# A recurrence stage on one core: VectorE's score spreading moved from behind the decay chain to ahead of it

## What is computed

```python
def step(state, inp):
    k_t, v_t, w_t, r_t = inp
    kv = k_t[..., :, None] * v_t[..., None, :]
    state = (1.0 - w_t)[..., :, None] * state + kv
    out = jnp.einsum('bhd,bhde->bhe', r_t, state)
    return (state, out)
...
y = outs.transpose(1, 0, 2, 3).reshape(Bv, Tv, Cv) @ Wo.T
x = x + y
...
# then, in the feed-forward part, a routing of each token on the signs of its normed row
tile_scores = input_sigs @ tile_sigs.T
tile_idx = jnp.argmax(jnp.where(in_cluster, tile_scores, -jnp.inf), axis=-1)
```

## Time and profile before

| | |
|---|---|
| time, median of 3 runs | 8956.1 us (8954.75 to 8961.61) |
| time of the profiled execution | 8956.13 us |
| its span | 8954.3 us |
| busy: PE, DVE, ACT, POOL | 7718.1 (86%), 7107.0 (79%), 4707.2 (53%), 5805.7 (65%) us |
| `core_phase` loop, 7107 to 8673 us: PE, DVE, ACT, POOL busy | 1241.11, 1350.70, 349.61, 755.26 us of 1566 |
| L1223 at 128x320, mean of 62 | 1534 ns |
| L1236, 124 instructions, mean | 690 ns |

### The profile page before, as it was taken

One profiled execution on the slowest core, in us unless ns is written; L12 is line 12 of the kernel. 1 busy time (PEld: TensorE's weight loads), 2 busy tenths in 40 slices (PEclk: granted clock), 3 DMA queues, 4 the chain that ended last, 5 costly groups with the idle time before them and its releaser, 6 DMA issues. The chain is left out here.

```text
span 8954.3 us, 223728 instructions
## 1 busy us (share of the span) xinstructions
PE 7718.1 (86%) x76550; PEld 5688.4 (64%) x76550; DVE 7107.0 (79%) x8782; ACT 4707.2 (53%) x10584; POOL 5805.7 (65%) x3304
## 2 busy tenths in 40 slices
PE   5659989999989899999999998899999877778774
PEld 3337777777777777777777776444444455555552
DVE  5549999999999999999999998323323488888876
ACT  4447777777777777777777776111111122222220
POOL 0019999999999999999999998000000144444444
PEclk8779999999999999999999999999999887777875
DMA  3340000000000000000000001122212211121115
GB/s 129 136 149 0 20 20 19 0 20 20 0 20 20 20 0 20 20 10 9 20 20 0 20 5 58 61 84 75 89 67 88 83 61 60 63 63 63 61 47 172
DMA packets 198781, 423.45 MB, mean 47 GB/s; under 512 B 22448, under 2 KB 48496, under 8 KB 183024
## 3 DMA queue, kind: packets, MB, share of 16 engines
q1 hardware_dynamic: 172768, 382.77, 12.7%
q10 hardware_dynamic: 25872, 38.80, 1.2%
HBM read 225.11 MB, written 196.41 MB: 47 GB/s over the span
## 5 line engine op out<-in xcount | busy, mean ns | idle before, releaser
L453 POOL TENSOR_TENSOR scan_hc<-scan_h,scan_cb 128x1024 f32<-128x1024 f32 x2048 | 4779.6, 2369 | 253.1 <-DMA scan_cb<-scratch_bc 117.6
L619 DVE TENSOR_TENSOR_SCAN scan_h<-scan_a,scan_carry,scan_u 128x512 f32<-128x512 f32 x4096 | 4801.9, 1261 | 156.1 <-PE scan_u L558 125.3
L558 PE MATMUL scan_u<-scan_dg,scan_v 64*128 64x128 f32 x32768 | 2391.7, 286 | 340.0 <-DVE scan_h L619 280.1
L504 ACT ACTIVATE scan_a<-scan_dt,scan_aneg 128x512 f32<-128x512 f32 x4096 | 2659.5, 708 | 44.4 <-issue 30.1
L558 PEld LDWEIGHTS scan_u<-scan_dg,scan_v 64*128 64x128 f32 x32768 | 2000.7, 188 | 820.0 <-DVE scan_h L619 538.1
L566 PE MATMUL scan_y<-scan_ident,scan_hc 128*128 128x128 f32 x16408 | 2250.4, 280 | 59.5 <-POOL scan_hc L453 33.6
L566 PEld LDWEIGHTS scan_y<-scan_ident,scan_hc 128*128 128x128 f32 x16408 | 1764.3, 141 | 309.7 <-POOL scan_hc L453 34.5
L475 ACT ACTIVATE scan_dg<-scan_half,scan_bt 128x64 f32<-128x64 f32 x4096 | 1138.7, 341 | 5.3 <-DVE scan_onward L602 5.2
L144 POOL TENSOR_TENSOR mid_r<-mid_ve,mid_half_neg 128x4 f32<-128x4 f32 x48 | 48.5, 1011 | 1269.0 <-DVE mid_ve L129 1269.0
L496 ACT ACTIVATE scan_carry<-scan_h,scan_onward 128x4 f32 (+1 forms) x1008 | 302.9, 301 | 1043.1 <-DVE scan_h L619 1043.1
L1223 DVE TENSOR_TENSOR core_rk<-core_rr,core_k 128x128 f32<-128x128 f32 (+7 forms) x512 | 409.0, 799 | 0.0
(11 more groups left out here) (211 smaller groups left out, 8209.8 us busy)
## 6 DMA issues: line engine op xcount, KB each, us to landing
scratch_y<-scan_yo ACTq DMA_DIRECT2D x17, 1024.0 KB, 4.7
pre_x<-in_x SPq DMA_DIRECT2D x16, 1024.0 KB, 6.9
scratch_z<-pre_zt SPq DMA_DIRECT2D x16, 1024.0 KB, 3.9
scratch_dt<-pre_dt SPq DMA_DIRECT2D x16, 1024.0 KB, 4.6
scratch_vr<-pre_vr ACTq DMA_DIRECT2D x16, 1024.0 KB, 4.7
scan_dt<-scratch_dt SPq DMA_DIRECT2D x16, 1024.0 KB, 5.3
scan_v<-scratch_vr SPq DMA_DIRECT2D x32, 512.0 KB, 7.7
scan_z<-scratch_z SPq DMA_DIRECT2D x16, 1024.0 KB, 10.7
```

The lines of the kernel that those rows point to most:

```text
L453: pool.tensor_tensor(hc[:, q].rearrange("p n (r j) -> p n r j", j=P), h[:, q].rearrange("p n (r j) -> p n r j", j=P), cb[:, bass.ds(b * NS ...
L504: ins = act.activation(a[:, q, n, :], dt[:, par, q, :], ACT.Exp, scale=aneg[:, q, bass.ds(m * 2 + n, 1)])
L558: mm = pe.matmul(u_ps[:, q % 2, g, k * HP:(k + 1) * HP, :], v[row, par, k, q, :], dg[row, buf, k], start=True, stop=True)
L619: ins = dve.tensor_tensor_scan(h[:, q, n, :], a[:, q, n, :], u_ps[:, q % 2, :, :, n].rearrange("p g t -> p (g t)"), carry[:, q, bass.ds(m ...
```

## The change

In VectorE's list `spread_scores`, with lead 2, is now written ahead of `decays`, with lead 3. Nothing else differs.

```diff
@@ -1259,7 +1259,7 @@
                 for e in range(2):
                     after.inc(dve.scalar_tensor_tensor(out=ext[:, e, :], in0=pen[:], scalar=mm2[:, e:e + 1], in1=ext[:, e, :], op0=ALU.min, op1=ALU.max))
                 after.wait(dve, i, after.n)
-            pipelined(dve, ITEMS, [(0, state), (0, norms), (3, decays), (2, spread_scores), (0, route)])
+            pipelined(dve, ITEMS, [(0, state), (0, norms), (2, spread_scores), (3, decays), (0, route)])
```

## The result

| | before | after |
|---|---|---|
| median | 8958.85 us (8954.75 to 8963.20, 4 runs) | 9076.86 us (9076.27 to 9077.90, 4 runs) |
| ratio | | 1.0132, 95% interval 1.0114 to 1.0149 |
| span of the profiled execution | 8954.3 us | 9076.1 us |

The change costs 118 us, 1.3%. The forecast was 9147 us with a range of 9070 to 9207; the measured time lies 7 us above the lower end.

The account below looks back on a forecast made before the run. VectorE's queue in the recurrence turn was taken as the bound. A 7.54 us wait, less 4.41 us, adds 3.13 us over 61 turns: 8956 + 191 = 9147 us, 2.1% slower, range 9070 to 9207 us.

Parts of the forecast that it names:

- The dependence: VectorE's moved L1236 must wait for TensorE's L1412, queued behind L1391, which waits for L1207 of the same turn.
- Part 2, what comes back: VectorE's decays, no longer slowed by GpSimd's products, fall from 11.47 to 6.98 us: 4.49 us back per turn.
- Part 3: Moved and unchanged work on VectorE: L1236 still 1.21 us, step to L1244 0.10 us, L1185 and L1191 gain margin.
- the earlier tree: TensorE's tree (L1361), no longer held by L1236, buys nothing: L1381 is held by the decays, L1391 by xf.
- The sum: From L1207's end to L1244, 12.70 us becomes 15.83: +3.13 us per turn, 61 turns, 191 us.
- Part 1, the mean wait: New VectorE wait before L1236 in each turn, the TensorE chain of 7.50 us plus 0.04: 7.54 us.
- TensorE's idle time before L1391 is what orders them: Chain lengths follow TensorE's prior idle time; with 5 to 11 us idle, the 29 turns' mean of 7.50 us applies.
- The lower bound: Smallest mean wait before L1236, 6.24 us, if every chain were like that of 7851.24.
- The signs: Profile after: L1236 waiting for L1412 about 62 times, 7 to 8 us each, some 460 us; turn about 28.5 us.
- The range: 8 in 10 range for the kernel's time, 9070 to 9207 us, lower end from a mean wait of 6.3 us.
- The rival of the lower clock: TensorE's chain always at the lower clock: wait 8.44 us, +4.03 us per turn, 9202 us; chance 0.12.
- The clock of the stage: TensorE's granted clock in the recurrence stage would be at or below 0.79.

Follow-up runs that it names:

- e1: Changed kernel with TensorE's L1412 (turn_scores) moved ahead of L1391 (turn_x): 8890.12 us, ratio 0.9924 to the kernel before.
- e4: Kernel before with GpSimd's keys cut in two, the first nine products run one item ahead: 8782.20 us, ratio 0.9805.
- e3: Changed kernel with an unread memset of 1024 columns added on VectorE behind L1236: 9227.60 us.
- e9: Changed kernel with an unread memset of 160 columns added on VectorE behind L1236: 9076.88 us.
- e10: Changed kernel without the second L1260 of route on VectorE, one instruction less per turn: 9073.82 us.
- e8: Kernel before with GpSimd's keys cut in two, TensorE's L1412 ahead of L1391 and L1236 ahead of the decays: 8708.48 us, ratio 0.9720.

## Why the prediction was right, and where it was off

- *The dependence.* Right: a new line of waits from L1412 to L1236, gone in e1.
- *Part 2, what comes back.* Right in cause and size: 6.96 us against the 6.98 of the sum. e1 and e4 show that the cause is GpSimd, from both sides.
- *Part 3.* Right: L1236 costs 1.21 us to the next start, the step to L1244 is 0.10. L1185 and L1191 wait for nothing on TensorE in the full turns. That the earlier tree bought nothing was not tested by itself; the sum comes out without it.
- *The sum.* Its form was right: 61 turns, wait minus 4.41 us. With the mean of the pair, 6.37, it gives +1.96 us per turn and 120 us; over all 61 turns, the first few included, the wait averages 6.41 us, which gives 122 us. Measured are 118, and 122 between the two spans.
- *Part 1, the mean wait.* This is the term that was mis-sized: 7.54 us forecast, 6.37 measured, 61 x 1.17 = 71 us, all of the miss. The step that failed is "TensorE's idle time before L1391 is what orders them". The idle time came out as forecast (8.0 and 8.5 us, forecast 5 to 11), and yet no steady chain was long; in e3 the same idle time, 8.96 us, goes with chains of 6.27 and of 8.40 us. The lower bound, 6.24 us, was near the truth. The signs moved with it: 406 us of waiting and not some 460, 6.3 to 6.5 us each and not 7 to 8, a turn of 27.3 us and not 28.5.
- *The range.* It held the time by 7 us, in part by luck. Its lower end goes back to a wait of 6.3 us, called the mean of the turns with less idle time. By the prediction's own figures that mean is 6.39 us for the chain and 6.43 for the wait, which gives 9079 us, just over the measured time.
- *The rival of the lower clock* (9202 us) did not come true in the changed kernel. Yet it is close: 1.06 us more work per turn brings the chain to 7.60 us on average (e3).
- The clock of the stage was to be at or under 0.79; it was 0.81, a small sign of the same error.

What I could have seen: in the kernel before, nothing waited for the end of the chain, a pair took 50.7 us and the place of the rise wandered through the turns. It came 3.3 us after the end of L1207 at 7800.54, 3.8 at 7851.24 and 4.8 at 7952.63, and not at all within the chain of 7825.64. So its 61 chains were a sample of many places. Once the chain is on the path that sets the turn, the turn answers to it, as e9 and e10 show, and the sample no longer holds.

## What to carry to other kernels

Before an instruction is moved up in one engine's queue, look at what it waits for and at what stands ahead of that in the releasing engine's queue: the same move lost 118 us behind one order of TensorE and won 68 us behind another. Where two engines interfere, put the instruction that is not slowed (here the one with its scores in PSUM) into the time of the interference. And when a wait on TensorE comes onto the path that sets a loop's turn, don't take its mean from a trace in which it was hidden.

## What the runs showed of the hardware

- The loop came to rest on the clock: with VectorE's work per turn changed by -0.19 to +0.19 us the pair of turns stayed at 54.60 to 54.62 us. How far it holds with less work than that was not tested. Outside that room 0.33 us of added work cost 38 us in all and 1.06 us cost 151, about twice what was added. What sets the time of the rise was not tested; only its place in the chain was seen, and that it comes at even steps of 27.3 us in the steady turns.
- Beside GpSimd's products a VectorE instruction of two columns (L1201) takes 0.77 us in the median, against 0.16 at the least, and L1207 up to 1.64 us (e4, e8), against 0.75. L1236, with its scores in PSUM and its mask in SBUF, takes its 0.69 us either way. The Trainium skill ("SBUF — State Buffer", section "SBUF: two separate sides") has a GpSimd instruction hold the shared ports against VectorE instructions with two SBUF inputs. e1 and e8 agree with that for L1236, which has one input there, and so does the 1.35 us of the first operation of the decays in e4: it ended at 7820.93, 0.14 us after GpSimd's product. By how much each kind of instruction is slowed only these rows tell.
